# A score unit that begins with its maximum in BF16, chunks behind that product, and denominators in four 32-column products

## The reference

```python
x = L0_attn_inputs                                   # (2, 2048, 256)
qkv = layernorm(x) @ W_qkv                            # 16 heads of 64
score = einsum('bihd,bjhd->bijh', q, k) / 8           # causal mask
out = einsum('bijh,bjhd->bihd', softmax(score, axis=2), v) @ W_out
x = x + out
lilora = up_aux @ (lora_up @ (lora_down @ down_aux))
x = x + layernorm(x) @ (W + lilora).T + b
```

## Time and profile before

| | |
|---|---|
| median of 3 runs | 1911.34 us (1908.52 to 1912.63) |
| the profiled execution, its own time | 1910.15 us |
| its span (first to last instruction) | 1908.1 us |
| granted TensorE clock, mean | 0.991 |
| PE busy | 1833.8 us (96%) |
| PEld busy | 1128.0 us (59%) |
| DVE busy | 1272.3 us (67%) |
| ACT busy | 806.7 us (42%) |
| POOL busy | 972.8 us (51%) |

### The profile page before, as it was taken

How to read it: one execution, slowest core, us unless ns; L and a number is a source line. 1 busy time by engine, 2 the same in 40 slices (tenths; PEclk the granted TensorE clock), 3 DMA queues, 4 the chain that set the end, 5 groups by cost and what they waited for, 6 DMA issues and landing times. The chain is left out here.

```text
span 1908.1 us, 34290 instructions
## 1 busy us (share of the span) xinstructions
PE 1833.8 (96%) x13464; PEld 1128.0 (59%) x13464; DVE 1272.3 (67%) x2123; ACT 806.7 (42%) x982; POOL 972.8 (51%) x532
## 2 busy tenths in 40 slices
PE   7999998999999999999999999999999999998998
PEld 5877776555555555555555555555555555554897
DVE  5364652868676767676776767686777676747565
ACT  3222123454545454545454454545454545454221
POOL 1011000666675858575665666666758585746211
PEclk9999998999999999999999999999999999998999
DMA  5646445212121212222121312121212121023551
GB/s 204 223 179 232 164 157 210 68 35 78 41 73 46 72 46 68 62 58 67 46 74 51 80 45 79 40 74 46 67 46 73 46 68 51 24 73 102 177 192 56
DMA packets 150782, 171.33 MB, mean 90 GB/s; under 512 B 44618, under 2 KB 91744, under 8 KB 150624
## 3 DMA queue, kind: packets, MB, share of 16 engines
q1 hardware_dynamic: 150624, 169.15, 28.0%
HBM read 97.02 MB, written 71.57 MB: 88 GB/s over the span
## 5 line engine op out<-in xcount | busy, mean ns | idle before, releaser
L1017 DVE TENSOR_REDUCE f_part_max<-b_ring 128x1 f32<-128x512 f32 (+3 forms) x1200 | 675.3, 604 | 317.5 <-PE b_ring L850 213.5
L948 ACT ACTIVATE b_probs<-b_scores 128x1024 f32<-128x1024 f32 (+3 forms) x640 | 567.4, 898 | 615.5 <-PE b_scores L822 357.9
L1123 POOL TENSOR_TENSOR b_sum_pool<-b_sum_pool,b_probs 128x1024 f32<-128x1024 f32 x237 | 569.2, 2402 | 32.1 <-POOL b_sum_pool L1123 0.5
L1123 POOL TENSOR_TENSOR b_sum_pool<-b_probs 128x1024 f32<-128x1024 f32 x48 | 115.7, 2411 | 324.8 <-DVE g_sum_dve L1049 308.7
L822 PE MATMUL b_scores<-f_split 64*128 64x512 f32 (+2 forms) x1920 | 269.5, 383 | 9.1 <-ACT b_probs L948 7.3
L822 PE MATMUL b_scores<-b_split 64*128 64x512 f32 (+2 forms) x1920 | 268.0, 381 | 3.3 <-ACT b_probs L948 3.1
L886 PE MATMUL b_o_acc<-b_probs,f_v_in 128*64 128x512 f32 (+3 forms) x1280 | 270.5, 544 | 0.0
L886 PE MATMUL b_o_acc<-b_probs,b_v_in 128*64 128x512 f32 (+3 forms) x1280 | 269.0, 541 | 0.7 <-ACT b_probs L948 0.7
L1049 DVE TENSOR_TENSOR g_sum_dve<-g_sum_dve,b_probs 128x768 f32<-128x768 f32 (+3 forms) x243 | 229.5, 944 | 34.1 <-ACT b_probs L948 26.1
L822 PEld LDWEIGHTS b_scores<-b_split 64*128 64x128 f32 x1920 | 165.6, 185 | 51.0 <-issue 20.4
L822 PEld LDWEIGHTS b_scores<-f_split 64*128 64x128 f32 x1920 | 168.2, 187 | 46.0 <-issue 19.4
(11 more groups left out here) (135 smaller groups left out, 2288.5 us busy)
## 6 DMA issues: line engine op xcount, KB each, us to landing
f_raw<-k_t SPq DMA_DIRECT2D x32, 512.0 KB, 4.8
f_raw<-q_t SPq DMA_DIRECT2D x32, 512.0 KB, 5.6
g_recip<-r_t SPq DMA_DIRECT2D x128, 128.0 KB, 3.0
o_t<-g_o_norm SPq DMA_DIRECT2D x64, 256.0 KB, 2.0
q_t<-a_stage_a SPq DMA_DIRECT2D x32, 256.0 KB, 2.4
q_t<-a_stage_d SPq DMA_DIRECT2D x32, 256.0 KB, 2.0
k_t<-a_stage_a SPq DMA_DIRECT2D x32, 256.0 KB, 2.0
k_t<-a_stage_d SPq DMA_DIRECT2D x32, 256.0 KB, 2.0
```

Source lines behind the costliest of these rows:

```text
L948: nc.scalar.activation(probs[s % PR][:, :, off:], scores[s % 2][:, :, off:], ACT.Exp, scale=scale).then_inc(exp_done, 1)
L1017: nc.vector.tensor_reduce(part_max[:, h, ib, c:c + 1], rowwise[h][:, 0:width], AX.X, ALU.max).then_inc(chunk_reduced, 1)
L1123: nc.gpsimd.tensor_tensor(sum_pool[:], first, probs[s % PR][:], ALU.add).then_inc(pool_added, 1)
```

## The change

The maximum is split into a BF16 high and a BF16 low row (`max_high`, `max_low`), which lie in two partitions of each head's half of a BF16 `shift`. The stationary operand is `first_rows`, BF16, with ones in two rows of each half. Its product becomes the first of a unit. Chunks of the first place stand behind this product (between), no longer ahead of the unit; those of the second place stay ahead of the second unit. In the plan "s.B" becomes ".sB" (steps 5 and 11). DVE makes the maxima with two operations instead of one, and SP places them with four DMAs instead of two. The denominators become four products of 32 stationary columns and 256 moving columns, each in a column quarter; ACT copies 256 instead of 512 columns, and four DMAs instead of two spread them. `wo_hi` has a buffer of its own.

```diff
+DEN = TILE // 2
-    nc.gpsimd.memset(halves(consts["first_row"][:]), 0.0).then_inc(filled, 1)
+    nc.gpsimd.memset(consts["first_rows"][:], 0.0).then_inc(filled, 1)
-        nc.gpsimd.memset(halves(consts["first_row"][h * H:h * H + 1, :]), 1.0).then_inc(filled, 1)
+        nc.gpsimd.memset(consts["first_rows"][h * H:h * H + 2, :], 1.0).then_inc(filled, 1)
...
             else:
-                want = "s.B" if t else "..B"
+                want = ".sB" if t else "..B"
...
-        shift = [lead["shift"], sb("shift1", [P, L], F32R)]
+        shift = [lead["shift"], sb("shift1", [P, L], BF16)]
...
                     wait_apart(sp, den_copied, n * TI + t + 2, o_stored, 1)
-                    for h in range(2):
-                        sp.dma_start(den_spread[:, h, :], den_row[h * D:h * D + 1, :].rearrange(
+                    for c in range(4):
+                        h, half = divmod(c, 2)
+                        sp.dma_start(den_spread[half * D:(half + 1) * D, h, :], den_row[c * P // 4:c * P // 4 + 1, :].rearrange(
                             "o (p i) -> o p i", i=NB)).then_inc(den_moved, 16)
...
                     for h in range(2):
-                        sp.dma_start(halves(shift[u][h * D:h * D + 1, :]).rearrange("o (b i) -> o b i", i=P),
-                                     halves(max_rows[h * KB:(h + 1) * KB, :])).then_inc(max_placed[u], 16)
+                        for i, rows in enumerate((max_high, max_low)):
+                            sp.dma_start(shift[u][h * D + i:h * D + i + 1, :].rearrange("o (b i) -> o b i", i=P),
+                                         rows[h * KB:(h + 1) * KB, :]).then_inc(max_placed[u], 16)
...
-                def score_unit(n, u, s):
+                def score_unit(n, u, s, between=()):
...
-                        pe.wait_ge(max_placed[u], (n - u) * 16 + 32)
+                        pe.wait_ge(max_placed[u], (n - u) * 32 + 64)
...
-                    for term, (a, b) in enumerate(((k_hi, q_hi), (k_hi, q_lo), (k_lo, q_hi), (None, shift))):
+                    for h in range(2):
+                        nc.tensor.matmul(scores[s % 2][:, h, lo:TILE], consts["first_rows"][head(h), :],
+                                         shift[u][head(h), queries], start=True, stop=False)
+                    for k in between:
+                        chunk(n + 1, 1 - u, k)
+                    for term, (a, b) in enumerate(((k_hi, q_hi), (k_hi, q_lo), (k_lo, q_hi))):
                         for h in range(2):
-                            lhs = consts["first_row"][head(h), :] if a is None else a[u][head(h), keys]
-                            last = nc.tensor.matmul(scores[s % 2][:, h, lo:TILE], lhs, b[u][head(h), queries],
-                                                    start=(term == 0), stop=(term == 3 and not diagonal))
+                            last = nc.tensor.matmul(scores[s % 2][:, h, lo:TILE], a[u][head(h), keys],
+                                                    b[u][head(h), queries], start=False,
+                                                    stop=(term == 2 and not diagonal))
...
-                    for h in range(2):
-                        last = nc.tensor.matmul(denom[head(h), :], consts["ones"][:, 0:D],
-                                                sum_dve[t % 2][:, h, :], start=True, stop=True)
+                    for c in range(4):
+                        h, half = divmod(c, 2)
+                        cols = slice(half * DEN, (half + 1) * DEN)
+                        last = nc.tensor.matmul(denom[c * P // 4:(c + 1) * P // 4, 0:DEN], consts["ones"][:, 0:P // 4],
+                                                sum_dve[t % 2][:, h, cols], start=True, stop=True)
...
                         for e in range(2):
-                            for k in places[e]:
-                                chunk(n + 1, 1 - u, k)
                             ahead = s + e + AHEAD
                             if ahead < U:
-                                score_unit(n, u, ahead)
+                                for k in places[1] if e else ():
+                                    chunk(n + 1, 1 - u, k)
+                                score_unit(n, u, ahead, () if e else places[0])
...
-                    denom = ring[:, ring_banks["denom", t][0], :]
+                    denom = ring[:, ring_banks["denom", t][0], 0:DEN]
                     nc.scalar.copy(den_row[:], denom).then_inc(den_copied, 1)
...
-                    nc.vector.tensor_copy(max_rows[:], ring[:, ring_banks["turn", 0][0], 0:P]
-                                          ).then_inc(max_rows_ready, 1)
+                    turned = ring[:, ring_banks["turn", 0][0], 0:P]
+                    nc.vector.tensor_copy(max_high[:], turned).then_inc(lead["max_high_ready"], 1)
+                    dve.wait_ge(lead["max_high_ready"], m + 1)
+                    nc.vector.tensor_tensor(max_low[:], turned, max_high[:], ALU.subtract).then_inc(max_rows_ready, 1)
...
-                "den_row": sb("den_row", [P, TILE]),
+                "den_row": sb("den_row", [P, DEN]),
-                "wo_hi": lead["shift"][:].rearrange("p (k n) -> p k n", n=cin),
+                "wo_hi": sb("wo_hi", [P, KC, cin], F32R),
```

More of the change, by code:

```diff
@@ L233, in place_first_max @@
                     for h in range(2):
-                        sp.dma_start(halves(shift[h * D:h * D + 1, :]).rearrange("o (b i) -> o b i", i=P),
-                                     halves(max_rows[h * KB:(h + 1) * KB, :])).then_inc(lead["max_placed"], 16)
+                        for i, rows in enumerate((max_high, max_low)):
+                            sp.dma_start(shift[h * D + i:h * D + i + 1, :].rearrange("o (b i) -> o b i", i=P),
+                                         rows[h * KB:(h + 1) * KB, :]).then_inc(lead["max_placed"], 16)
                 def tile(T, u, ahead):
@@ L491, in _ @@
                 make_constants(nc, pool, consts, constants)
-                nc.gpsimd.memset(halves(shift[:]), 0.0).then_inc(lead["shift_cleared"], 1)
+                nc.gpsimd.memset(shift[:], 0.0).then_inc(lead["shift_cleared"], 1)
                 for p in range(LOADS):
@@ L903, in item @@
                         places = plan[s // 2] if following else ((), (), ())
+                        assert s + AHEAD < U or not any(places)
                         for e in range(2):
-                            for k in places[e]:
-                                chunk(n + 1, 1 - u, k)
                             ahead = s + e + AHEAD
                             if ahead < U:
-                                score_unit(n, u, ahead)
+                                for k in places[1] if e else ():
+                                    chunk(n + 1, 1 - u, k)
+                                score_unit(n, u, ahead, () if e else places[0])
                             elif following:
@@ L1130, in _ @@
                 pool.sem_inc(o_ready, 2)
-                nc.gpsimd.memset(halves(shift[1][:]), 0.0).then_inc(shift_cleared, 1)
+                nc.gpsimd.memset(shift[1][:], 0.0).then_inc(shift_cleared, 1)
                 for n in range(2 * PAIRS):
@@ L1248, in finish_last_o @@
                     sp.wait_ge(tail["den_copied"], o_tiles + 1)
-                    for h in range(2):
-                        sp.dma_start(tail["den_spread"][:, h, :], tail["den_row"][h * P // 2:h * P // 2 + 1, :].rearrange(
-                            "o (p i) -> o p i", i=NB)).then_inc(tail["den_moved"], 16)
+                    for c in range(4):
+                        h, half = divmod(c, 2)
+                        sp.dma_start(tail["den_spread"][half * P // 2:(half + 1) * P // 2, h, :],
+                                     tail["den_row"][c * P // 4:c * P // 4 + 1, :].rearrange("o (p i) -> o p i", i=NB)
+                                     ).then_inc(tail["den_moved"], 16)
                     sp.wait_ge(tail["inverted"], o_tiles)
@@ L1338, in _ @@
                 pe.wait_ge(tail["dve_added"], tail["dve_ops"])
-                for h in range(2):
-                    half = slice(h * P // 2, (h + 1) * P // 2)
-                    last = nc.tensor.matmul(last_denom[half, :], consts["ones"][:, 0:P // 2],
-                                            tail["sum_dve"][last_t % 2][:, h, :], start=True, stop=True)
+                for c in range(4):
+                    h, half = divmod(c, 2)
+                    cols = slice(half * DEN, (half + 1) * DEN)
+                    last = nc.tensor.matmul(last_denom[c * P // 4:(c + 1) * P // 4, :], consts["ones"][:, 0:P // 4],
+                                            tail["sum_dve"][last_t % 2][:, h, cols], start=True, stop=True)
                 last.then_inc(tail["denom_made"], 1)
@@ L1378, in _ @@
                 act.wait_ge(tail["denom_made"], o_tiles)
-                act.wait_ge(tail["den_moved"], (o_tiles - 1) * 32 + 1)
+                act.wait_ge(tail["den_moved"], (o_tiles - 1) * 64 + 1)
```

(9 more changed lines are left out.)

18 lines of the change are left out of this document (11 added, 7 removed).

## The result

| | before | after |
|---|---|---|
| median, same chip (4 runs each) | 1910.89 us | 1931.37 us (1926.89 to 1931.61) |
| ratio to before, 95% interval | | 1.0102 (1.0084 to 1.0121) |
| the profiled execution, its span | 1910.15, 1908.1 | 1931.61, 1929.5 |
| granted TensorE clock, mean | 0.991 | 0.980 |

The kernel became 20.5 us slower; 1908.7 was forecast. Its median there lay between 1909.2 and 1910.9 us, so a difference of two medians from different chips can be off by some 2 us; where it matters, the difference by the ratios stands beside it.

What follows compares the result with a forecast made beforehand. PE was taken to set the pace, busy 87.97 of 89.71 us per item. Terms of -1.3, +0.64, +1.58, -1.1 and +0.1 for the maxima, with -1.1 in the last item, gave 1908.7 us, own range 1902 to 1915, chance 0.50.

Steps and rivals of the forecast that it cites:

- the sum +1.58: Steps 4, 5, 10 and 11: the moved DVE addition delays the last chunks, +1.58 us per item.
- a granted clock that falls in these waits: Sign of a wrong prediction in the profile after: the clock falls in PE's waits; no size or chance given.
- The BF16 product: First product of a unit: shorter weight loads behind shape changes and mask products, 512-column pair 0.215; -1.3 us per item.
- Chunks behind the product: Eight steps with a second-place chunk: +0.125 us each, less 0.095 in four, 0.02 for step 16; +0.64 per item.
- step 17, booked as -0.20: Step 17, with a first-place chunk and no second one behind: the BF16 first product gains 0.20 us.
- Quarters: Denominators: four quarters run at a time, 0.58 us instead of 0.86, four times an item; -1.1 us per item.
- The rival of 1936: Denominators: quarters run two at a time, each group costs +0.15 instead of -0.28 us; 1936 us, chance 0.18.
- The rival "doesn't bind" (1887): Steps 5 and 11: the moved addition slips into DVE's pauses, so 1.45 us doesn't arise; 1887 us, chance 0.16.
- The maxima and the spreading DMAs: Maxima's cover is 0.26 us thin, +0.1 per item; two more spreading DMAs delay the inverse by 1.1, hidden.
- POOL's late place: The inverse, delayed 1.1 us by two more spreading DMAs, stays hidden because POOL needs it late.

Runs made afterwards that it cites:

- e3: The changed kernel with eight repeated, useless products of head 0 in the wait before the last chunks of steps 5 and 11; 1908.85 us, ratio 0.9996.
- e7: The kernel before with nothing changed but the plan string, the small chunk of steps 5 and 11 in the second place; 1936.13 us, ratio 1.0140.
- e5: The changed kernel with the old plan string and all first-place chunks ahead of the unit again; 1882.26 us, ratio 0.9858.
- e2: The changed kernel with first-place chunks ahead of the unit again, the BF16 product still first in the unit; 1919.52 us, ratio 1.0047.
- e1: The changed kernel with the old plan string ("s.B") in the diagonal steps, all else changed; 1891.34 us, ratio 0.9895.
- e6: The changed kernel with the old plan, a chunk behind the BF16 product only where no second-place chunk follows; 1882.84 us, ratio 0.9855.
- e12: The kernel e6 with DVE's inversion of the denominators one unit later; 1900.53 us, ratio 0.9954.

## Why the prediction was wrong, step by step

**The step that failed** is the sentence "what PE gains in steps 4 and 5 is only longer wait, all of it now in front of step 5's last chunk", and with it the sum +1.58. It priced the wait at full clock. The wait itself was sized about right: without most of the falls (e3 against before) it cost +0.98 in steps 4 and 5 together where +0.67 stood, and +0.71 in steps 10 and 11 where 0.91 stood, 1.69 in sum against 1.58. The clock behind it was priced at nothing, without a reason given, and it cost 22.5 us by e3 (20 by the ratios). The prediction named "a granted clock that falls in these waits" among the signs of being wrong, but gave it no price, no place among the rivals and no chance. The rest holds roughly: with the clock kept up, e3 measured 1908.85, and 1908.7 was forecast for a change that does not touch the clock. So close a match is luck. An item of e3 is 0.24 us longer than one of before where 0.1 less was forecast, which is 5 us in fifteen items; steps 16 and 17 are 0.24 of that difference. The profiled run of e3 took 1911.15, not 2.6 less than before's 1910.15 but 1.0 more.

**The rows that were there.** The earlier trace rows show a wait of 2.49 before, at an undisturbed clock, and I took that as harmless. e7 shows the same wait of 2.49 with work at half clock behind it. One long wait without a fall was no evidence for 30 of them.

**The BF16 product.** The prediction was right about its place behind a change of shape: the first pair ends 0.322 after PV in the matmul records where 0.335 was worked out; its weights take 94 ns. It was right about its place behind mask products, where the 0.08 is gone: a 256-column pair ends 0.109 behind the masks in e5, and an FP32R one 0.200 in before. It was slightly wrong about the stream: a 512-column BF16 pair takes 0.232, like FP32R, not 0.215. With the quarters, steps 2, 6 and 12 gained 0.50, 0.43 and 0.40 in e3, where 0.20 + 0.28 stood.

**Chunks behind the product.** Right: +0.12 in steps 3, 7, 9 and 13 (0.125), +0.03 in steps 8, 14 and 15 (0.03). Step 16 cost 0.13 where 0.05 stood, and step 17, booked as -0.20, gained 0.04: there too the chunk behind the product waits for the chunk before it. By e2, and by e5 against e1, this part costs 9 to 12 us, so it was not worth its place.

**Quarters.** Right: four at a time. The eight records add 0.569 us where halves added 0.858; 0.58 was forecast. By the Trainium skill, TensorE: Matmul & The Clock Gate, Measured speedup vs the span model, three column tiles give a speedup of 2.38, so they overlap less than fully. This trace doesn't show that for four FP32 quarters: the four of the second round start 0.24 us behind those of the first, and the measured 0.569 includes the change of shape. The rival of 1936 was near the measured time for a wrong reason.

**DVE's order.** The rival "doesn't bind" (1887) fell: e7 and e1 both show that it binds. e1's 1891 lies near that number, but with the old order.

**The maxima and the spreading DMAs.** PE idles in step 19 for 0.06 us an item after the change, in e3 for nothing and in e5 for 0.14, where 0.1 was booked; the profile doesn't name what it waited for. The two more spreading DMAs are nearly hidden after the change: DVE waits for them in 7 places, four of them in the last item. The other three, 1.5 us together, stand in step 5, in the items with the three longest waits of PE (3.00, 2.77 and 2.32). In the faster e6 DVE waits in 21 places. So the cover comes, it seems, from PE's own delay and not from POOL's late place, as the prediction had it; no run tests that by itself.

## What to carry to other kernels

Price a wait on TensorE together with the clock behind it. Waits of under 1.5 us were free of that here, but for one in e3. Gathered into pieces of 1.2 to 3.0 us they were followed by half clock in 14 of 30 places, and that cost as much again as the order that made the waits (20 to 22.5 us against 17 to 19, from e3 and e1). Where such a wait can't be removed, useless products in it can pay (20 to 22.5 us here), but undoing the order that gathered it paid more (40 us). And a change of five parts is to be run part by part: here one string of a plan hid a gain of 1%, and the placement of the chunks another 0.4%.

## What the runs showed that I had not expected

The length of a wait does not decide by itself. After the change, idles of 1.75 in item 6 and 1.77 in item 7, both in step 11, were followed by clocks of 1.00 and 0.57; the six of 1.16 to 1.48 all by 1.00; in e1 29 windows with idles of at most 1.48 stayed at 1.00, and the one behind 1.60 fell; in e6 three of 1.73, 1.85 and 2.09 stayed at 1.00. The one fall in items 0 to 14 of e3 came behind an idle of 0.92, what the filler had left of a longer wait. In the last item the denominators' wait of 2.49 left the clock up in before and not in e7. What else decides stays open; no run here tells it. The mean clock barely varies from run to run of one kernel, though: it was 0.979 to 0.981 in the four runs of the change and 0.977 to 0.978 in those of e2.

An addition on DVE of 1.22 us takes up to 2.2 us when POOL works beside it. Of the 48 such additions of e12 (line 1073), 26 had POOL idle and took 1.22 to 1.23 us, and the 22 with POOL at work took 2.18 to 2.21. So what POOL does is part of DVE's times even where neither waits for the other.
